# Softmax attention block on one Trainium2 core: the diagonal copies of the transposed probabilities go from DMA to ScalarE and GpSimd, residual loads and bias adds move, and the start is reordered

## What is computed

```
h   = group_norm(x, scale, bias)             # per batch, 32 groups
qkv = h @ qkv_w + qkv_b
q, k, v = split(qkv, 3)                      # each (16, 1024, 512)
q = (q / sqrt(sqrt(64))).reshape(16 * 8, 1024, 64)   # one "head" = 128 tokens x 8 chunks
k = (k / sqrt(sqrt(64))).reshape(16 * 8, 1024, 64)
v = v.reshape(16 * 8, 1024, 64)
a = softmax(q @ k^T) @ v                     # 1024 x 1024 per head
out = x + a.reshape(16, 1024, 512) @ proj_w + proj_b
```

## Time and profile before

| | us |
|---|---|
| median of 3 runs | 3390.11 (3389.07 to 3390.60) |
| the profiled execution | 3395.64 |
| its span, first to last instruction | 3393.9 |
| busy: PE, DVE, ACT, POOL | 3299.0, 2890.4, 2011.1, 1647.7 |
| granted PE clock, mean | 0.997 of full |
| DMA engines, mean busy share | 0.75 to 0.8 through the run |

### The profile page before, as it was taken

The page is one execution under the profiler, slowest core; times in us unless marked ns, Lnnn a source line. Parts: engine busy times, 40 slices in busy tenths (PEclk is TensorE's granted clock), DMA queues, the critical chain, the costliest instruction groups (busy, mean ns, idle before and its releaser), DMA issues.

```text
span 3393.9 us, 66911 instructions
## 1 busy us (share of the span) xinstructions
PE 3299.0 (97%) x24128; PEld 2488.8 (73%) x24128; DVE 2890.4 (85%) x3601; ACT 2011.1 (59%) x3857; POOL 1647.7 (49%) x2762
## 2 busy tenths in 40 slices
PE   4999999999999999999999999999999999999998
PEld 3777777777777777777777777777777777777775
DVE  4888888888888888888888888888888888888886
ACT  3565665655655656656566566566566565665663
POOL 3454545544545545455445455454454554554552
PEclk9999999999999999999999999999999999999999
DMA  4777878788787877878878788787878878788777
GB/s 94 191 190 191 203 183 203 186 196 201 185 201 185 199 192 186 202 189 196 197 191 202 187 197 194 191 200 188 202 186 194 199 184 200 191 200 194 186 187 181
DMA packets 311097, 646.84 MB, mean 191 GB/s; under 512 B 80112, under 2 KB 145648, under 8 KB 310768
## 3 DMA queue, kind: packets, MB, share of 16 engines
q1 hardware_dynamic: 290992, 604.82, 74.7%
q10 hardware_dynamic: 19776, 37.76, 3.3%
HBM read 71.84 MB, written 33.55 MB: 31 GB/s over the span
## 4 chain that ended last, share of the span: by engine, by line
PE 58%; SPq 26%; DVE 5%; ACT 4%; issue 3%; DMA 2%; POOL 1%; DVEq 0%; POOLq 0%; ACTq 0%
SPq L310 22%; PE pv_ps L372 15%; PE s_ps L343 15%; PE c_ps L408 5%; PE c_ps L409 5%; PE c_ps L410 5%; SPq L291 3%; DVE turned L605 2%; PE c_ps L422 2%; PE c_ps L424 2%; PE c_ps L423 2%; ACT probs L465 2%; ACT staged L485 2%; PE c_ps L390 2%; PE c_ps L391 2%
## 5 line engine op out<-in xcount | busy, mean ns | idle before, releaser
L465 ACT ACTIVATE probs<-s_ps,neg_max 128x1024 f32<-128x1024 f32 x1024 | 1141.0, 1115 | 827.6 <-DVE neg_max L622 824.6
L622 DVE TENSOR_REDUCE neg_max<-s_ps 128x1 f32<-128x1024 f32 x1024 | 1204.6, 1218 | 271.1 <-PE s_ps L343 270.5
L605 DVE STREAM_TRANSPOSE turned<-probs 128x1024 f32<-128x1024 f32 x1024 | 1232.5, 1228 | 126.3 <-ACT probs L465 72.6
L372 PE MATMUL pv_ps<-probs_t,v 128*64 128x256 f32 x8192 | 943.3, 383 | 6.3 <-DMA probs_t<-turned 6.3
L372 PEld LDWEIGHTS pv_ps<-probs_t,v 128*64 128x64 f32 x8192 | 566.9, 137 | 358.3 <-issue 95.0
L408 PE MATMUL c_ps<-h_hi,w_hi 128*128 128x256 f32 x2048 | 594.5, 290 | 28.8 <-DVE x_res L643 10.0
L485 ACT ACTIVATE staged<-c_ps,qk_bias 64x256 f32<-64x256 f32 x1024 | 481.4, 470 | 188.4 <-PE c_ps L410 175.2
L409 PE MATMUL c_ps<-h_lo,w_hi 128*128 128x256 f32 x2048 | 580.1, 283 | 0.0
L410 PE MATMUL c_ps<-h_hi,w_lo 128*128 128x256 f32 x2048 | 579.4, 283 | 0.0
L781 POOL COPY inv_wide<-inv_sum 128x256 f32<-128x256 f32 x256 | 101.7, 397 | 829.9 <-PE pv_ps L354 822.1
L408 PEld LDWEIGHTS c_ps<-h_hi,w_hi 128*128 128x128 f32 x2048 | 392.6, 192 | 39.8 <-DVE x_res L643 14.0
(11 more groups left out here) (68 smaller groups left out, 5044.1 us busy)
## 6 DMA issues: line engine op xcount, KB each, us to landing
probs_t<-turned SPq DMA_DIRECT2D x4096, 128.0 KB, 2.4
x_res<-in_x SPq DMA_DIRECT2D x128, 256.0 KB, 3.0
result<-x_res ACTq DMA_DIRECT2D x128, 256.0 KB, 3.0
x_next<-in_x SPq DMA_DIRECT2D x480, 64.0 KB, 2.1
probs_t<-in_L_conv_qkv_w ACTq DMA_DIRECT2D x16, 192.0 KB, 9.5
turned<-in_x SPq DMA_DIRECT2D x16, 128.0 KB, 10.9
probs_t<-in_L_conv_proj_w ACTq DMA_DIRECT2D x4, 256.0 KB, 14.6
v_bias<-in_L_conv_qkv_b SPq DMA_DIRECT2D x1, 256.0 KB, 7.6
```

The lines of the kernel that those rows point to most:

```text
L372: last = nc.tensor.matmul(pv_ps[side][CH * par:CH * (par + 1), 0, :], v_sb[:, ring_of(i, parity), CH * chunk:CH * (chunk + 1)], p_t[:, par ...
L465: nc.scalar.activation(probs[k % 2][:, :], s_ps[k % 2][:, :], ACT.Exp, bias=neg_max[:, k % 4:k % 4 + 1], accum_out=row_sum[:, (k // HALF) ...
L605: nc.vector.transpose(dst, probs[k % 2][:, :].rearrange("p (k b j) -> p k b j", k=CHUNKS, b=QUADS)).then_inc(probs_turned, 1)
L622: nc.vector.tensor_reduce(neg_max[:, k % 4:k % 4 + 1], s_ps[k % 2][:, :], AX.X, ALU.max, negate=True).then_inc(max_ready, 1)
```

## The change

1. **Diagonal copies.** `move_half` issues 12 DMAs for a half and no longer 16. Quadrants 2 and 3 are copied by ACT (in its step m = 2, 6, 10, 14, behind that step's two exponentials), quadrants 0 and 1 by POOL, at the head of its program for the step of four slots behind the half. Consumers wait for the two new semaphores too.
2. **The residual.** SP loads at m = 1 and m = 9, two slots later, and POOL's `add_bias` goes from the programs of m = 0 and m = 8 into those of m = 4 and m = 12, behind the two copies.
3. **The start.** The first batch's x goes ahead of all weights: two groups of it by SP, two by ACT. Then SP loads the weights by their k, q and v columns (48 DMAs of 32 x 512) and proj_w, ACT the vectors and biases. Rounding and splitting follow in the same order (k, q, v), proj_w's in slots 0 and 2 of the first batch. The first pair's tiles are made in the order 4, 5, 6, 7, 0, 1, 2, 3, and the first scores wait for as many tiles as they read: five for slots 0 and 1, then one more for every two slots.

The core of the diff:

```diff
-                for step in range(QUADS):
+                for step in range(1, QUADS):
                     for a in range(QUADS):
                         to = (a + step) % QUADS
                         sp.dma_start(probs_t[n % 2][Q * to:Q * (to + 1), a, :],
...
-                if k % 16 == 7:
+                if k % 16 == 1:
+                    load_residual(b, 2 * (k // 16) - 2)
+                if k % 16 == 9:
                     load_residual(b, 2 * (k // 16) - 1)
-                if k % 16 == 15:
-                    load_residual(b, 2 * (k // 16))
...
+            def keep_quadrants(b, k):            # ACT
+                n = (k - KEEP_LAG) // HALF       # KEEP_LAG = 6
+                half = 2 * BLOCKS * b + n
+                act.wait_ge(probs_turned, HALF * half + HALF)
+                at_least(act, pv_done, half - 1)
+                for a in (2, 3):
+                    quad = slice(Q * a, Q * (a + 1))
+                    nc.scalar.copy(probs_t[n % 2][quad, a, :], turned[n % 2][quad, a, :]).then_inc(kept_act, 1)
...
+            def keep_quadrants(b, k):            # POOL
+                n = k // HALF - 1
...
+                pool.wait_ge(probs_turned, HALF * half + HALF)
+                at_least(pool, pv_done, half - 1)
+                pool.wait_ge(inv_widened, half + 1)
...
+                for a in (0, 1):
+                    quad = slice(Q * a, Q * (a + 1))
+                    at_least(pool, kept_pool, 2 * half + a)
+                    nc.gpsimd.tensor_copy(probs_t[n % 2][quad, a, :], turned[n % 2][quad, a, :]).then_inc(kept_pool, 1)
+                pool.wait_ge(kept_pool, 2 * half + 2)
...
             def four_slots(b, k):
                 m, pair = k % 16, k // 16
+                keep_quadrants(b, k)
+                if m == 4:
+                    add_bias(b, 2 * pair - 2)
+                if m == 12:
+                    add_bias(b, 2 * pair - 1)
...
-                if m == 0:
-                    add_bias(b, 2 * pair - 2)
...
-                if m == 8:
-                    add_bias(b, 2 * pair - 1)
...
+            for n in range(2):
+                load_x_start(sp, n)
+            for part in (1, 0, 2):
+                for t in range(KT):
+                    load_weight_rows(sp, part, t)
+            for t in range(KT):
+                sp.dma_start(pw_stage[t], proj_w[t * P:(t + 1) * P, :]).then_inc(pw_loaded, 16)
...
+                if g == 0 and i == 0:
+                    pe.wait_ge(qk_ready, START_TILES.index(c // 2) + 1)
+                elif k % 16 == 0:
                     pe.wait_ge(qk_ready, 2 * KT * (g + 1))
```

More of the change, by code:

```diff
@@ L268, in _, with load_weight_rows @@
         def _(sp):
-            def broadcast_row(row):
-                return row.rearrange("(a n) -> a n", a=1).broadcast_to([P, C])
-            for n in range(PPB):
+            def load_weight_rows(sp, part, t):
+                cols = slice(part * C, (part + 1) * C)
                 for z in range(QUADS):
[L274 to L284, removed]
+                    rows = qkv_w[P * z + Q * t:P * z + Q * (t + 1), cols]
+                    sp.dma_start(w_stage[t][Q * z:Q * (z + 1), cols], rows).then_inc(w_loaded[part], 16)
+            for n in range(2):
[5 more added lines that the diff above has]
+                sp.dma_start(pw_stage[t], proj_w[t * P:(t + 1) * P, :]).then_inc(pw_loaded, 16)
             def load_x_tile(b, u):
@@ L400, in make_qk @@
                     pe.wait_ge(w_ready, 1)
[L401 removed]
+                if before_start(b) and n == KT:
                     pe.wait_ge(w_ready, 2)
@@ L549, in step @@
                     norm_x(b, k, 1)
[L550 to L560 removed]
+                if before_start(b) and k == GROUP_VAR_SLOT:
+                    round_qkv_weights(1)
+                    round_qkv_weights(0)
+                if before_start(b) and k == GROUP_VAR_SLOT + 4:
+                    round_qkv_weights(2)
+                if b == 0 and k == 0:
+                    round_proj_weights()
+            for n in range(2, PPB):
+                load_x_start(act, n)
+            with nc.allow_non_contiguous_dma("vectors to the partitions, once"):
+                for vector, row in ((n_scale, norm_scale), (n_bias, norm_bias)):
+                    for z in range(QUADS):
+                        act.dma_start(vector[Q * z:Q * (z + 1), :], row[P * z:P * (z + 1)].rearrange("(t j) -> j t", j=Q)
+                                      ).then_inc(const_loaded, 16)
+                act.dma_start(qk_bias[:, :], qkv_b[0:2 * C].rearrange("(j p) -> p j", p=P)).then_inc(const_loaded, 16)
+            for bias, row in ((v_bias, qkv_b[2 * C:3 * C]), (p_bias, proj_b)):
+                act.dma_start(bias[:, :], row.rearrange("(a n) -> a n", a=1).broadcast_to([P, C])).then_inc(wide_loaded, 16)
             batches(in_steps(step))
@@ L668, in step @@
                     scale_bias()
-                    for part in range(3):
-                        split_qkv_weights(part)
-                    split_proj_weights()
+                    split_qkv_weights(1)
+                    split_qkv_weights(0)
+                if before_start(b) and k == GROUP_VAR_SLOT + 4:
+                    split_qkv_weights(2)
             def statistics(b, k):
```

58 lines of the change are left out of this document (42 added, 16 removed).

## The result

| | before | after |
|---|---|---|
| median of 4 runs | 3390.18 (3389.07 to 3390.60) | 3442.09 (3440.86 to 3442.44) |
| the profiled execution | 3395.64 | 3442.44 |
| its span | 3393.9 | 3440.7 |

The changed kernel is slower: ratio 1.0153, 95% interval 1.014 to 1.0166. The forecast was 3411 (3372 to 3428): the right side, and 31 us too little.

A forecast was written before the change was run, and what follows sets the result against it. PE bounds the kernel, without holes in the steady state, so only the start, the end and a few PE waits can give time. -14 + 58 - 18.2 - 2.5 - 2.6 = +21 us, so 3411; range 3372 to 3428.

The forecast's parts named there:

- The chain of m = 4: POOL's inv_wide, two copies, bias, DVE's take-out, PE's qk 1: PE loses 0.94 us, 62 times, +58 us.
- The copy's price: One POOL copy of 32 x 1024, called c: 1.06 us by the slope of the trace rows.
- The rival of the other sign, a cheap copy: POOL's copy on 32 partitions costs up to 0.6 us, so the bias is in time: 3353; chance 0.17.
- blocking with DVE: POOL's two copies each wait for half a DVE transpose: 74 us more, 3485; chance 0.04.
- ACT's copies: Two copies of 1024 floats behind ACT's exponentials: costed at 0, at most 0.4 us a pair, +26.
- The late take-outs: DVE's bank take-outs, late behind SP's moves, held up PE's weight loads; their end was worth -14 us.
- the rival in which the weights land late: At the start, q weights land 8 us late through SP; start worth 10 less, 3421; chance 0.12.
- the start and first pair: Up to pair 1's first v product: first scores at 46.6 (-18.2), first pair -2.5; together -20.7 us.
- Now five tiles are needed: First q/k matmul to first scores: three q tiles fewer, plus 1.5 for PE's pace: -5.4 us.
- I take 4.5 off, and 2 on for proj_w's parts: First pair: fewer waits for SP's moves, but proj_w's parts added: -2.5 us, bounds -7 and +2.
- the end: Last pair: last moves start on time (-2.1) and are 12 (-2.5), DVE waits for bias (+2): -2.6 us.
- The base: Terms added to the profiled 3395.64 give 3417; less 5.5, its distance above the median 3390.11, gives 3411.

The follow-up runs named there:

- e1: Changed kernel with POOL's bias add ahead of its two copies at m = 4 and m = 12; 3365.43 us, ratio 0.9936.
- e3: Changed kernel with one POOL copy instead of two, quadrant 1 by DMA again (13 moves a half); 3368.49 us, ratio 0.9945.
- e6: Changed kernel with the bias add ahead of the copies at m = 4 only; 3366.93 us in one run.
- e7: e1 with the scores of slots 0 and 1 ahead of the eighth q/k tile in PE's program; 3362.55 us, ratio 0.9924.
- e5: e1 with proj_w's rounding and splitting moved back before the first batch; 3360.96 us, ratio 0.992.
- e10: Kernel before with the copies on ACT and POOL alone; residual, bias and start as they were; 3376.94 us, ratio 0.9962.
- e2: Changed kernel with all 16 moves by DMA and no ACT or POOL copies, residual and start as changed; 3390.25 us, ratio 1.0009.
- e11: e2 with residual and bias where they were before, so the new start alone; 3380.24 us, ratio 0.9971.

## Why the prediction was right and wrong

**Right: the mechanism and its sign.** The chain of m = 4 was the largest term, in the right place, 62 times, ending in PE's qk 1 (e1, e3, e6). The copy's price was right: c = 1.06 forecast, 1.037 measured. The rival of the other sign, a cheap copy, is out: 32 partitions save nothing. The Trainium skill (GPSIMD Engine Reference, Architecture) says that each core has its own 16 partitions; the trace agrees, with 1.037 us for 1024 floats on 32 partitions. No blocking with DVE: its transposes take 1229 ns on average where they took 1228, its maxima 1219 where they took 1218. ACT's copies cost the ordinary pairs nothing (e1), nor does m = 12 (e6). The late take-outs gave back 14.8 (forecast 14). The statistics ended at 22.9 (21.7), the first q/k matmul came at 31.91 (31). That matmul waited for POOL's split of h, so the rival in which the weights land late is out too.

**Wrong, +15: the chain's loss was 0.94 and is 1.18.** "An instruction that waits for the one before starts 0.08 after its end" was read from a cast and its follower. Behind `inv_wide` the copies wait 0.22 (+0.14); the two copies and their gaps took 0.06 less than forecast, the bias and its gap 0.02 more, the take-out's lead over qk 1 was 0.75 and not 0.71 (+0.04), and behind the wait PE's second matmul starts 0.22 after the first, where 0.12 is usual: 0.10 more. Each is a tenth or so, and 62 x 0.24 = 14.9. A chain that is repeated in every pair multiplies the error of each link.

**Wrong, +9.6: the start and first pair gave 11.1 of 20.7.** Two steps failed. "Now five tiles are needed ... 21.0 - 3 x 2.3 = 14.1": I counted which tiles the scores need, and not what stands ahead of them in PE's program. The first scores missed the forecast by 6.0. Of this 0.9 is the first q/k matmul, and 5.1 the way from there: 20.72 us and not 15.6. e7 removed the obstacle, and there it takes 15.69. So the 5.4 was what five tiles are worth, with PE's pace in it, but only in a program that lets the scores go ahead; as the kernel was, it gave 0.3. About 1 us of any start is PE's speed: the first tiles' matmuls follow each other at 0.21 us, as they do where the granted clock is given as 0.50 (in e1 from 48.50 to 55.30), and later at 0.12. The change came at 40.42 in the changed kernel and at 38.30 in e1, and e1's fifth tile was ready 0.9 sooner (47.15). The profile gives no lower clock for these first tiles; that it was the clock is read from the pace.

```profile
40.01 0.41 PE L420 MATMUL c_ps<-h_lo,w_hi 128*128 128x256 f32 x1
...
40.42 0.28 PE L419 MATMUL c_ps<-h_hi,w_hi 128*128 128x256 f32 x1
...
38.30 0.28 PE L421 MATMUL c_ps<-h_hi,w_lo 128*128 128x256 f32 x1
```

The second step is "I take 4.5 off, and 2 on for proj_w's parts": the first pair became 1.2 longer. The parts cost 2.2 there (e5), so about 1.1 came of the 4.5, and copies alone shorten that pair by 1.2 (e10). The 4.5 rested on "SP's moves kept DVE waiting in part of the 7.1 us left". The waits of before's first pair (67.1 to 116.7) put that at one wait of 0.4 us; the rest DVE waited for PE and ACT, 2.2 us of it for exponentials:

```profile
DVE turned L605 <- ACT probs L465: 2.2, 3, 0.9
...
DVE turned L605 <- DMA probs_t<-turned: 0.4, 1, 0.4
```

**Wrong, +2.1: the end gave 0.5 of 2.6.** Up to the end of DVE's last transposes the last pair is 2.4 longer, 45.6 for 43.3 (forecast +2). The moves themselves were priced right: SP ends them 7.5 us behind these transposes, where it was 12.2, 4.6 less. But from the transposes to the end only 2.9 came off: with the moves out of the way PE waited for something else, 3.02 us for ACT's copies, which the forecast had put at nothing. With the bias first the whole last pair is 65.2 instead of 68.96.

**The base: 5.** I took 5.5 off because before's profiled execution lay that far above its median; the changed kernel's (3442.44) lies at its own. The offset belonged to the one execution, not to both kernels. The kernels with 16 moves spread widely from run to run (before by 6.0, 5.8 and 8.9 us in 13, 7 and 9 runs, e2 by 10.4 in 10, e11 by 8.6 in 6), those with 12 by 0.6 to 2.8 in four each. More runs spread further, and before itself spread by 1.5 in the four of the result; that late moves cause the rest was not tested by itself.

Misses: 15 + 9.6 + 2.1 + 5 = 31.7, less 0.8 for the late take-outs: the 31 us. None of them turns the sign: with the chain's loss as measured, 73, and all gains as forecast, 37 with the last pair's +2 taken in, the kernel is still slower. All four erred to the same side, which is chance; nothing ties the one of the base to the others.

## What to carry to other kernels

Before an instruction is put into an engine's program between two others, list who waits for what is queued behind it: here a copy that nobody needed for microseconds stood ahead of a bias that PE waited for, and two swapped calls were worth about 75 us. When a wait is relaxed, look for what stands ahead of it in the waiting engine's own program; the wait may not be what ends last. And price every link of a chain that repeats per iteration, the gap behind each wait and the restart of the last engine among them, since a tenth of a us comes back 62 times.

## What the runs showed of the hardware

- POOL copies 32 x 1024 floats in 1.037 us and 128 x 256, as many floats, in 0.397: the time goes by the floats of a partition. ACT takes 1.044 for the same copy.
- POOL's copies stood 0.22 us behind the end of `inv_wide`, and a split 0.08 behind the cast that it needs; the difference between the two was not examined.
- POOL's copies on 32 partitions beside DVE's transposes and maxima did not lengthen these: 1229 and 1219 ns on average, before 1228 and 1218.
- The granted clock stood at half (0.50 and 0.51 in the two rows of e5 above) in stretches of the start and the end, and where such a stretch fell differed between traces of nearly the same program. Landmarks of the first and the last pair are good to about 1 us for that; ordinary pairs, at a granted clock of 1.00, repeat to 0.02.
- In e10 SP waited long and without harm to PE:

```profile
SPq L301 <- DMA result<-x_res: 427.6, 127, 5.8
```

Before it was 127.0 us in 54 waits. In all SP waited for other engines and stores for about 982 us in e10 and 246 before, where its late moves reached PE 19 times; in e10 they did so not once.
